# Causal scores on Trainium2: which engine adds the mask of the second block of queries

## What is computed

```python
x = x + _L0_attn_ref(_layernorm(x, axis=-1), Wq, Wk, Wv, Wo, bo)
# inside, per batch and head:
s = jnp.einsum('bqhd,bkhd->bhqk', q * scale, k)
causal = jnp.tril(jnp.ones((t, t), dtype=bool))
s = jnp.where(causal[None, None], s, -jnp.inf)
p = jax.nn.softmax(s, axis=-1)
o = jnp.einsum('bhqk,bkhd->bqhd', p, v)
```

## Time and profile before

| what | value |
|---|---|
| median of 3 executions | 513.3 us (513.06 to 515.04) |
| the profiled execution, its time | 513.02 us |
| the profiled execution, its span | 511.3 us |
| mean granted TensorE clock | 0.975 of full |
| TensorE matmul busy | 461.2 us, 90% of the span |
| VectorE busy | 412.7 us, 81% |
| ScalarE busy | 362.0 us, 71% |
| GpSimd busy | 288.4 us, 56% |
| chain that ended last | PE 55%, DVE 31%, issue 5%, ACT 4%, DMA 4% |
| attention steps with VectorE masks | about 48 to 337 us |
| feed-forward part | about 360 us to the end |

### The profile page before, as it was taken

How to read it: one execution, slowest core, us unless ns; L and a number is a source line. 1 busy time by engine, 2 the same in 40 slices (tenths; PEclk the granted TensorE clock), 3 DMA queues, 4 the chain that set the end, 5 groups by cost and what they waited for, 6 DMA issues and landing times.

```text
span 511.3 us, 14335 instructions
## 1 busy us (share of the span) xinstructions
PE 461.2 (90%) x4105; PEld 325.4 (64%) x4105; DVE 412.7 (81%) x1518; ACT 362.0 (71%) x782; POOL 288.4 (56%) x583
## 2 busy tenths in 40 slices
PE   2878999999999999999999989978999999999990
PEld 1635566566455555655655645534999899999980
DVE  5978789999989989998998999893677775558885
ACT  8575778677777767777786866777677667777660
POOL 5612545444566575675676666457765774545541
PEclk9868999999999999999999999999999999999996
DMA  8334233232233334324324323573222332236653
GB/s 225 105 105 115 85 101 87 86 95 83 82 102 93 96 96 115 98 77 126 100 72 121 107 78 90 164 209 79 73 82 77 99 100 76 65 81 190 184 176 104
DMA packets 49837, 54.92 MB, mean 107 GB/s; under 512 B 6947, under 2 KB 41937, under 8 KB 49760
## 3 DMA queue, kind: packets, MB, share of 16 engines
q1 hardware_dynamic: 45120, 45.18, 31.3%
q0 software_dynamic: 4320, 8.47, 4.9%
q10 hardware_dynamic: 320, 0.36, 0.2%
HBM read 34.96 MB, written 17.90 MB: 103 GB/s over the span
## 4 chain that ended last, share of the span: by engine, by line
PE 55%; DVE 31%; issue 5%; ACT 4%; DMA 4%; SPq 1%; POOL 1%; DVEq 0%; POOLq 0%; ACTq 0%
PE psO L1013 13%; DVE psS L1323 11%; PE psT L1172 9%; DVE maxs L1326 7%; PE psS L983 7%; PE psO L1183 6%; PE psM L1183 6%; PE psT L996 3%; PE psS L1172 3%; DVE maxs L1323 2%; PE psS L1162 2%; PE psM L1023 1%; DVE attn L1337 1%; ACT PT L797 1%; PE psS L986 1%
## 5 line engine op out<-in xcount | busy, mean ns | idle before, releaser
L797 ACT ACTIVATE PT<-psT 128x512 f32<-128x512 f32 x320 | 172.2, 597 | 72.9 <-PE psO L1013 48.4
L1323 DVE CUSTOM_DVE_ANT_0 psS<-mask_row,psS 128x512 f32<-128x512 bf16 (+1 forms) x232 | 142.6, 623 | 28.9 <-PE psS L983 28.0
L983 PE MATMUL psS<-Ks,Qs 96*128 96x128 bf16 (+3 forms) x512 | 133.9, 310 | 13.1 <-DVE maxs L1326 7.8
L598 POOL TENSOR_SCALAR_AFFINE_SELECT PT<-PT 128x512 f32<-128x512 f32 x128 | 79.2, 633 | 100.7 <-ACT PT L797 100.2
L996 PE MATMUL psT<-Qs,Ks 108*128 108x384 bf16 (+3 forms) x512 | 109.0, 300 | 3.4 <-ACT PT L797 2.6
L680 POOL DMA_INDIRECT token_y<-Qs,y_row x71 | 70.3, 990 | 55.4 <-DVE Qs L1717 45.4
L983 PEld LDWEIGHTS psS<-Ks,Qs 96*128 96x128 bf16 x512 | 50.6, 99 | 58.5 <-DVE maxs L1326 27.5
L1326 DVE TENSOR_REDUCE maxs<-psS 128x2 f32<-128x512 f32 (+3 forms) x120 | 76.4, 668 | 4.7 <-PE psS L986 3.9
L1013 PE MATMUL psO<-PT,Vs 128*32 128x512 f32 (+3 forms) x1024 | 75.9, 436 | 1.2 <-DVE x_all L1349 1.1
L629 POOL DMA_INDIRECT sorted_x<-xn,place x64 | 64.6, 1009 | 18.8 <-issue 16.4
L996 PEld LDWEIGHTS psT<-Qs,Ks 108*128 108x128 bf16 x512 | 43.7, 97 | 30.1 <-ACT PT L797 11.7
(11 more groups left out here) (256 smaller groups left out, 736.0 us busy)
## 6 DMA issues: line engine op xcount, KB each, us to landing
Qs<-q_parts SPq DMA_DIRECT2D x96, 96.0 KB
Ks<-k_parts SPq DMA_DIRECT2D x95, 96.0 KB
xs_t<-sorted_x SPq DMA_DIRECT2D x71, 65.0 KB
w_sb<-in_L_ffn_w SPq DMA_DIRECT2D x16, 256.0 KB
q_parts<-qparts SPq DMA_DIRECT2D x32, 96.0 KB, 2.4
k_parts<-kparts SPq DMA_DIRECT2D x8, 384.0 KB, 2.7
x_all<-in_L_attn_x SPq DMA_DIRECT2D x8, 256.0 KB, 4.8
v_all<-token_y SPq DMA_DIRECT2D x4, 512.0 KB, 4.3
```

The source lines that it names most:

```text
L598: pool.affine_select(out=square, in_=square, compare_op=ALU.is_ge, fill=0.0, base=0, pattern=[[0, GH], [1, P]], channel_multiplier=-1).the ...
L797: act.activation(PT[:, n * T:(n + 1) * T], psT[:, bank, :], ACT.Exp).then_inc(prob_done[bank], 1)
L983: last = pe.matmul(psS[:, bank, c0:c0 + n], Qs[0:QK_ROWS, g, h, j * P:n], Ks[0:QK_ROWS, g, h, 0:n], start=True, stop=alone)
L1323: dve.tensor_tensor_reduce(src, mask_row[:, (CH - 1 - j) * P:], src, 1.0, NEG, ALU.add, ALU.max, maxs[:, par, j, h:h + 1]).then_inc(scores ...
```

## The change

In the tasks of query block j = 1 (a = 9 and 10, two heads each), TensorE no longer adds the mask, from s = 3 on. VectorE does it there, as in the tasks of one head: one `tensor_tensor_reduce` over 256 columns for each of the two heads, where one `tensor_reduce` over both heads stood. The bank is released after the second. Task 8 (j = 0, four heads) and all tasks of the steps 0 to 2 stay as they are.

```diff
                 for j, h, c0 in SCORE_TASKS[a]:
                     n = (j + 1) * P
-                    alone = len(SCORE_TASKS[a]) == 1 and s >= PE_MASKED
+                    alone = len(SCORE_TASKS[a]) < GH and s >= PE_MASKED
                     last = pe.matmul(psS[:, bank, c0:c0 + n], Qs[0:QK_ROWS, g, h, j * P:n], Ks[0:QK_ROWS, g, h, 0:n],
                                      start=True, stop=alone)
                     if not alone:
...
                 dve.wait_ge(scores_ready[bank], turn + 1)
                 (j, h, _), heads = SCORE_TASKS[a][0], len(SCORE_TASKS[a])
-                src = psS[:, bank, 0:(j + 1) * P * heads]
-                if heads > 1:
-                    src = src.rearrange("p (h n) -> p h n", h=heads)
-
-                if heads == 1 and s >= PE_MASKED:
-                    dve.tensor_tensor_reduce(src, mask_row[:, (CH - 1 - j) * P:], src, 1.0, NEG, ALU.add, ALU.max,
-                                             maxs[:, par, j, h:h + 1]).then_inc(scores_used[bank], 1)
+
+                if heads < GH and s >= PE_MASKED:
+                    for j, h, c0 in SCORE_TASKS[a]:
+                        src = psS[:, bank, c0:c0 + (j + 1) * P]
+                        last = dve.tensor_tensor_reduce(src, mask_row[:, (CH - 1 - j) * P:], src, 1.0, NEG, ALU.add, ALU.max,
+                                                        maxs[:, par, j, h:h + 1])
                 else:
-                    dve.tensor_reduce(maxs[:, par, j, h:h + heads], src, AX_X, ALU.max).then_inc(scores_used[bank], 1)
+                    src = psS[:, bank, 0:(j + 1) * P * heads].rearrange("p (h n) -> p h n", h=heads)
+                    last = dve.tensor_reduce(maxs[:, par, j, h:h + heads], src, AX_X, ALU.max)
+                last.then_inc(scores_used[bank], 1)
```

## The result

The changed kernel takes 519.2 us (median of 8 runs, 517.0 to 520.9) against 513.4 us for the kernel before in the same comparison: a ratio of 1.0098, 95% interval 1.008 to 1.0117. A second comparison gave 1.0075 (1.0053 to 1.0097). It is slower by 4 to 6 us. The forecast was 520.1 us and 6.8 us slower, in a range of 515.8 to 524.2.

What follows compares the result with a forecast made beforehand. TensorE and VectorE together close the attention loop, with VectorE's tasks 9 and 10 on the path. Terms 6.1 + 0.8 + 0.5 - 0.6 = 6.8 us on 513.02 made 519.8, as median 520.1; range 515.8 to 524.2.

Steps and rivals of the forecast that it cites:

- The price of VectorE's two tasks: VectorE, start of task 9 to end of task 10: 1.62 us instead of 1.28, 0.34 us more.
- The third rival: VectorE's next custom starts only after the readout before it: 23 us slower, 536 us; chance 0.04.
- Both tasks on the path in 18 steps: Where the chain runs through VectorE to task 10's end, both tasks count in full: 18 x 0.34 = 6.1 us.
- Task 10 would be done in time: Five g = 1 steps, chain leaving VectorE after task 9: only task 9 counts, 5 x 0.15 = 0.8 us.
- g = 2, named as the test: Distance between `weigh`s in g = 2 steps up by 0.3 us; the prediction is wrong if they don't lengthen.
- the wait at `turn_shift`: In s = 10, 14, 18 and 22 a later `weigh` hides 0.15 us of waiting for GpSimd: 0.6 us back.
- small shifts: Small VectorE instructions in a step: the sum is off if they shift by more than 0.1 us a step.
- the extra is absorbed: VectorE's idle time or better-placed small instructions take up the extra: 513.3 + 0 to 2.5 us; chance 0.08.
- costed at nothing outside g = 0: The 7.0 us of mask matmuls removed from TensorE gain nothing outside g = 0, covered by its wait for VectorE.
- g = 0: Five steps where the chain shows TensorE with VectorE close behind: 0.1 us longer on average, 0.5 us in all.

Runs made afterwards that it cites:

- experiment 4: The changed kernel with the changed tasks 9 and 10 only in the steps of g = 2, all other steps as before; ratio 0.9999 to the kernel before.
- second profiles: The kernel before and the changed kernel each run and profiled once more, nothing altered; ratio of changed to before 1.0075.
- experiment 1: The kernel before without TensorE's mask matmuls of tasks 9 and 10 from s = 3 on, VectorE's reduces unchanged; 510.5 us, ratio 0.9919.
- experiment 2: The changed kernel with TensorE's masks put back and VectorE's customs of 256 columns adding zeros; 519.7 us, ratio 1.0097 to the kernel before.
- experiment 6: The kernel before with no masks in the first pass on either engine from s = 3 on, all 11 tasks with one plain reduce; ratio 0.9949.
- experiment 10: The changed kernel with task 8's masks on VectorE too, four customs of 128 columns for one reduce; 542.3 us, ratio 1.0518 to the kernel before.

## Why the prediction was right, and where it was not

**Direction, size and range** held: 4 to 6 us slower where 6.8 was forecast. The main reason held too: tasks 9 and 10 stand at the end of VectorE's part, and their higher price is paid there. But the sum was 2 us too high, and one sign that the prediction had named as its own test, the g = 2 steps, came out against it. Term by term:

**The price of VectorE's two tasks** was exact: 0.34 and 0.38 us for each custom and 1.62 us for both tasks, from the straight line through two widths. The Trainium skill's price by columns (VectorE: DVE Perf Modes, "The TRN2 errata") was 0.39 for 256 and 0.66 for 512 columns; the trace has 0.34 to 0.38 and, for the reduce, 0.60. The third rival, customs that pay in full, is out by the rows above: a readout and the next custom start together. The Trainium skill's rule that the next instruction waits for an empty pipeline (VectorE: DVE Perf Modes, "The DRAIN you can't avoid") does not hold between these two; the same section says itself that an instruction which is not held starts earlier, with which these rows agree.

**Both tasks on the path in 18 steps** held in g = 3 and in s = 24, 25 and 28 in the main: g = 3 is 0.27 us longer on average. Three of its steps (s = 3, 7 and 27) got 0.29 to 0.31 longer. In s = 7 and 27 a small instruction stands between the two tasks, which makes their price 0.30 instead of 0.34 (experiment 4). s = 11, 19 and 23 got only 0.18 to 0.19 longer, because the late start of task 3 is gone from them. s = 15 got 0.42 (0.43 in the second profiles), and I have no reason for it. Step 29, booked with 0.34, took 8.36 us in both kernels.

**"Task 10 would be done in time" in g = 1** is a step that failed. I booked 0.15 us for each of five steps; they got 0.16 to 0.30 longer, 0.26 on the mean. The rows of step 13 show it: the readout of task 10 ends at 179.72, and score task 2 starts at 179.78, so task 10 is what it waits for. From the start of task 9 it was 178.78 - 177.38 = 1.40 us to score task 2, and is 179.78 - 178.10 = 1.68, 0.28 more: nearly the whole 0.34, less what task 10 had in hand before. Also task 9 alone counts to the end of its readout, 0.34 + 0.38 + 0.14 = 0.86 against 0.68, so 0.18 and not 0.15.

**g = 2, named as the test** ("it is wrong if the steps of g = 2 don't lengthen"), did not lengthen: the four usual ones went from 9.81 to 9.71 and s = 2 from 9.38 to 9.26; only s = 6 and 26 got longer, by 0.08 and 0.10. This is the term that was mis-sized most: 6 x 0.34 - 0.6 = 1.4 us forecast, 0.3 us less than before measured. The mechanism was there, 0.30 us of VectorE's, and two things paid for it: the wait at `turn_shift`, which I had booked at 0.15 a step and which gave 0.19, and the hold of `near` behind GpSimd, 0.22 us, which the profile of before showed (0.37 us for an instruction that is listed with 0.15 elsewhere) and which I had filed under small shifts. In s = 6 and 26 only the second is there, 0.30 - 0.22 = 0.08. The rival "the extra is absorbed" had named small instructions that are held; in the steps of g = 2 it came true in part. The chain of the changed kernel at the end of step 14, which answers to the earlier trace rows:

```profile
188.53 0.01 DVE near L1389
188.55 0.10 DVE rest L1443
...
189.37 0.07 DVE maxs L1322
189.44 0.05 issue
189.49 0.39 PE psS L983
```

It still runs through VectorE to the end of task 10 and straight on to score task 2. And `turn_shift` is no longer late, which answers to the earlier trace rows:

```profile
182.46 0.20 PE psM L1023 x4
```

**TensorE's saving "costed at nothing outside g = 0"** was too low. It is worth 2.2 us alone (experiment 1) and 1.8 beside VectorE's bill (experiment 2), and of the latter g = 0 has only 0.1. In g = 2 of experiment 1 the path is indirect: masks gone, the `probs` behind them and so ScalarE and GpSimd run 0.12 us earlier, and the hold of `near` ends as much earlier (0.37 to 0.26 us).

**g = 0** held in its number: 0.15 us longer on average; forecast were 0.1 in five steps and 0.34 in two, 0.17. Its reason did not: TensorE was to give back 0.24 us there, and experiment 2, without that saving, has these steps only 0.02 longer than the changed kernel.

By groups, g = 0, 1, 2, 3, the terms of the sum for the 28 steps were 1.2 + 1.4 + 1.4 + 2.4 = 6.4 us; measured were 1.0 + 1.8 - 0.3 + 1.9 = 4.4. Most of the 2.0 us lies in g = 2; g = 1 and g = 3 are off by 0.4 and 0.5 in opposite directions and nearly cancel, which is luck.

**A version that beats both.** Experiments 1 and 6 do, by 0.8% and 0.5%. They take the maximum over some keys that are masked later. The shift that it gives is never below the true maximum, and the softmax divides it out again, so the result is the same as long as the surplus is too small for the exponentials to vanish. This is a condition on the data; the kernels with masks have none.

## What to carry to other kernels

When two engines alternate within a step, ask which of them the end of the step waits for: work moved onto it just there is paid nearly in full where nothing else gives way (here 0.28 to 0.31 us a step of a price of 0.30 to 0.34), and what the other engine saves may come back in part (here about a third). Price a width that the trace lacks by a line through two it has, start to start rather than by the listed durations, and count one readout at the end of every wait. Before calling a small instruction free, compare its listed time with its own in other places: one listed with 0.37 us here and 0.15 there may be waiting for something, and may pay for a part of the change.

## What the runs showed of the hardware

- TensorE's clock fell from 1.00 to 0.50 during `weigh` after stretches in which TensorE had been busy for 1.57 or 1.76 of 3 us. The cost was 1.7 us for each `weigh` (4.01 instead of 2.36 us), five times what the extra VectorE work of such a step cost itself. But stretches with 1.76 (steps 11 and 23 of experiment 10), 1.54 and even 1.16 us (ahead of the last `weigh`s in the second profile of the changed kernel and the first of the kernel before) left it at 1.00, so what decides is open. With VectorE's part of the step another 0.34 us longer, six steps of the attention had it (experiment 10); experiment 6 had it in two; in the kernel before and the changed one the clock was full in all 28, in two profiles each.
- A small VectorE instruction with two SBUF inputs (`near` or `square`, 4 columns) was held until the running GpSimd mask ended, 0.25 to 0.53 us listed instead of 0.15, whereas the customs and reduces on PSUM beside the same masks kept their time.
- A custom behind a readout takes 0.65, 0.51, 0.38 and 0.25 us start to start for 512, 384, 256 and 128 columns, and behind anything else 0.04 to 0.05 less; the readout (0.14 us) starts together with it.
- Steps repeat to about 0.1 us between two profiles of one kernel, with one exception of 0.2, and their sum to 0.1 us, while the whole times spread over 4 us: a change of a per cent is better read from the steps.
